# A transformer layer on one core: the expert stretch moved from the 64th to the 80th key block, and the last group's preparation moved up on POOL

## What is computed

```python
xn = layernorm(x)
# attention: 16 heads of 16 numbers, rotary position terms on q and k
q, k, v = rope(xn @ Wq.T) * 16 ** -0.5, rope(xn @ Wk.T), xn @ Wv.T
attn = softmax(where(key > query, -inf, q @ k.T)) @ v
# feed-forward: 32 experts of 128 hidden numbers, 6 of them for each row, and a shared one
w, idx = gate(xn)                      # top 4 of 8 groups, then top 6 experts
y = sum over the 6: w * (silu(xn @ w11[e].T) * (xn @ w33[e].T)) @ w22[e].T
shared = (silu(xn @ sw1.T) * (xn @ sw3.T)) @ sw2.T
out = x + attn @ Wout.T + y + shared
```

## Time and profile before

| | us |
|---|---|
| median of three runs | 979.25 (975.77 to 980.76) |
| the profiled execution, its own time | 968.93 |
| its span in the trace, first to last instruction | 967.2 |
| PE busy | 871.4 |
| DVE busy | 627.8 |
| POOL busy | 525.4 |
| ACT busy | 503.7 |
| mean granted clock of TensorE, share of full speed | 0.959 |

### The profile page before, as it was taken

One profiled execution on the slowest core, in us unless ns is written; L12 is line 12 of the kernel. 1 busy time (PEld: TensorE's weight loads), 2 busy tenths in 40 slices (PEclk: granted clock), 3 DMA queues, 4 the chain that ended last, 5 costly groups with the idle time before them and its releaser, 6 DMA issues.

```text
span 967.2 us, 18271 instructions
## 1 busy us (share of the span) xinstructions
PE 871.4 (90%) x5601; PEld 480.7 (50%) x5602; DVE 627.8 (65%) x1285; ACT 503.7 (52%) x1206; POOL 525.4 (54%) x712
## 2 busy tenths in 40 slices
PE   5788856788999989989999999989999999999997
PEld 3445434333343434367888888854434354443344
DVE  3867665778866687855555555546687867878422
ACT  2322216244666656644444444546666677666662
POOL 2202227968998805236666666628886887830000
PEclk9989877779999999999999999989999999999998
DMA  7000001000000000117777877855552352520011
GB/s 207 1 25 25 25 4 49 17 1 1 1 2 1 2 1 14 37 41 237 218 236 224 237 221 236 135 119 72 72 73 40 49 73 33 72 39 1 6 39 44
DMA packets 55932, 70.93 MB, mean 73 GB/s; under 512 B 11552, under 2 KB 47392, under 8 KB 55840
## 3 DMA queue, kind: packets, MB, share of 16 engines
q0 software_dynamic: 19968, 31.47, 18.3%
q1 hardware_dynamic: 18976, 21.53, 7.4%
q10 hardware_dynamic: 16896, 16.78, 5.1%
HBM read 48.53 MB, written 21.23 MB: 72 GB/s over the span
## 4 chain that ended last, share of the span: by engine, by line
PE 72%; DVE 15%; ACT 4%; issue 3%; DMA 3%; DVEq 2%; SPq 0%; ACTq 0%
PE bank L1116 14%; PE bank L1101 11%; PE vector_banks L1181 11%; PE vector_banks L1081 11%; DVE mpart L886 8%; PE vector_banks L972 7%; PE bank L1194 5%; PE vector_banks L991 3%; PE bank L972 3%; DMA xn_all<-wexp 2%; ACT turned L570 2%; PE bank L991 2%; ACT probs L658 2%; PE vector_banks L1136 2%; PE vector_banks L1084 1%
## 5 line engine op out<-in xcount | busy, mean ns | idle before, releaser
L658 ACT ACTIVATE probs<-bank 128x512 f32<-128x512 f32 (+3 forms) x640 | 312.9, 534 | 221.4 <-PE bank L1101 107.1
L886 DVE TENSOR_REDUCE mpart<-vector_banks 128x2 f32<-128x1024 f32 (+3 forms) x320 | 326.7, 1061 | 93.9 <-PE vector_banks L1081 57.1
L1101 PE MATMUL bank<-turned 99*128 99x512 bf16 (+3 forms) x640 | 208.2, 357 | 13.0 <-ACT probs L658 5.4
L1081 PE MATMUL vector_banks<-turned 96*128 96x512 bf16 (+3 forms) x640 | 185.3, 361 | 17.0 <-DVE mpart L886 13.6
L538 POOL DMA_INDIRECT turned<-normed_rows,tok_i x128 | 125.3, 979 | 90.5 <-PE vector_banks L972 75.9
L553 POOL DMA_INDIRECT res<-expert_rows,slot_i x96 | 148.5, 1547 | 40.0 <-issue 29.9
L1116 PE MATMUL bank<-probs,V 128*32 128x512 f32 (+3 forms) x1280 | 152.6, 547 | 1.6 <-ACT probs L658 1.3
L1101 PEld LDWEIGHTS bank<-turned 99*128 99x128 bf16 x640 | 58.7, 98 | 179.2 <-ACT probs L658 109.3
L1181 PE MATMUL vector_banks<-xn_all,probs 128*128 x512 | 135.3, 387 | 3.5 <-issue 1.5
L484 POOL CAST cat_q<-qk_all 128x512 bf16<-128x512 f32 (+1 forms) x30 | 17.2, 688 | 146.5 <-DVE qk_all L732 98.1
L1181 PEld LDWEIGHTS vector_banks<-xn_all,probs 128*128 128x128 f32 x512 | 87.1, 190 | 16.1 <-issue 8.1
(11 more groups left out here) (153 smaller groups left out, 1003.6 us busy)
## 6 DMA issues: line engine op xcount, KB each, us to landing
expert_rows<-probs ACTq DMA_DIRECT2D x32, 512.0 KB, 4.1
xn_all<-wexp SPq DMA_DIRECT2D x32, 384.0 KB, 4.1
normed_rows<-xn_all SPq DMA_DIRECT2D x4, 512.0 KB, 3.1
turned<-normed_rows,tok_i POOLq DMA_INDIRECT x128, 3.8
out<-res SPq DMA_DIRECT2D x16, 128.0 KB, 1.7
res<-x SPq DMA_DIRECT2D x1, 1536.0 KB, 8.8
res<-expert_rows,slot_i POOLq DMA_INDIRECT x96
probs<-wqkvT SPq DMA_DIRECT2D x1, 768.0 KB, 5.6
```

Source lines behind the costliest of these rows:

```text
L658: A(PT[v // 2 % 4][:, v % 2, 0:width], bank[A_BANK[step][0]][:, 0:width], ACT.Exp).then_inc(s["scalar_bank_read"], 1)
L886: V.tensor_reduce(mpart[:, t % TPC, 2 * j:2 * j + 2, p], ring[:, :, 0:w], AX.X, ALU.max).then_inc(s["vector_bank_read"], 1)
L1081: last = mm(ring[:, h, 0:w], q_turned(slice(0, KQ), 2 * j + h, t * P, P), k_turned(par, slice(0, KQ), 2 * j + h, p * CH, w), start=True, s ...
L1101: last = mm(ring[:, 0:CH - off], k_turned(parity(g), slice(0, KM), h, kb * P, P), q_turned(slice(0, KM), h, c * CH + off, CH - off), start ...
```

## The change

The stretch of expert tiles is put in front of group 2, chunk 0 (block 80) in place of group 1, chunk 3 (block 64). On POOL the first half of group 3 is prepared after the combining of four tiles in place of eight, and the second half after eight in place of twelve. Nothing else changes; the waits inside `prepare_next` and `combine` stay as they are.

```diff
-EXPERTS_AT = (1, NCH - 1)
+EXPERTS_AT = (2, 0)
...
             combine(range(0, 4))
+            prepare_next(3, 0)
             combine(range(4, 8))
-            prepare_next(3, 0)
+            prepare_next(3, 1)
             combine(range(8, 12))
-            prepare_next(3, 1)
             combine(range(12, 16))
```

## The result

The changed kernel takes 986.67 us (median of ten runs, 980.72 to 989.13), the kernel before 977.82 in ten runs taken with them. The ratio is 1.0088, with a 95% interval from 1.0066 to 1.0111: slower by 8.6 us. The prediction was 986.

A forecast was written before the change was run, and what follows sets the result against it. PE was taken to bound the kernel, with POOL's preparation deciding at block 115. POOL's lateness +5.9, clock +1.9 and catching up -0.5 gave +7.3 us on a span of 967.2; 986 us was forecast, eight in ten 978 to 991.

The forecast's parts named there:

- A: Likeliest case: POOL late by 4 to 8 us at block 115, costing +4.5 to +9 us; chance 0.53.
- the restart: PE resuming attention behind the expert stretch: a 4.9 us cost, moved unchanged to blocks 80 to 83, so net 0.
- the wait: At block 115 PE waits 5.8 us for POOL's second half of group 3, ready at 123.6 against 117.8.
- catching up: Behind the wait at block 115, ACT and DVE have caught up on their work, worth 0.5 us gained.
- change of group: ACT's copy of the next values falls into the stretch's start, where ACT has nothing to do: -0.7 us.
- the clock: Behind the wait at block 115, PE's clock falls after idling, costing 1.9 us.
- B: Rival: POOL late by 1 to 3 us, both gaps behind the casts short; +1 to +4, about 982; chance 0.20.
- C: Rival: no wait at block 115, as the gap goes or PE comes slower; -2 to +2, about 979; chance 0.14.
- D: Rival: POOL later still, both gaps long, and the clock; +9 to +13, about 990; chance 0.07.
- E: Rival: restart absorbed in blocks 80 to 83, 4.8 us gained, about 974, if POOL issues transfers faster; chance 0.06.
- Entry: At block 80, before the stretch, DVE's longer last reduces delay the division and PE's first row turn: +0.8 us.
- The expert stretch: The stretch itself, 221.0 us from first row turn to first score step, was expected to keep its length.

The follow-up runs named there:

- second profile: The changed kernel run once more unchanged as a control, against the kernel before: ratio 1.0096, with a 4.96 us wait at block 115.
- the run with the first half sooner: Changed kernel with POOL preparing group 3's first half before its wait for the last expert rows and the combining: 975.13 us, 1.0025 to the kernel before.
- the last experiment: New POOL order and ACT's later store wait at block 64, 969.69 us; beside it, first half prepared before combining plus that wait at block 80, 970.12 us.

## Why the prediction was right

**What held.** The likeliest case, A, came about, by its own steps.

| step | predicted | measured, changed kernel |
|---|---|---|
| first transfer behind the restart | 3.61 | 4.78 |
| last issue of 24 to the first half's end | 18.8 | 17.1 |
| the same, second half | 15.0 | 15.0 |
| restart to second half ready | 123.6 | 122.9 |
| PE at block 115 behind the restart | 117.8 | 117.5 |
| the wait | 5.8 | 5.54 |
| behind the wait, clock less catching up | +1.4 | +2.1 (second profile +1.45) |
| blocks 80 to 83, restart less change of group | +4.2 | +3.3 (second profile +5.2) |

The restart-to-ready time is 826.82 less 703.95; PE's arrival is 826.96 less 5.54 less 703.95. In the second profile POOL was ready at 123.8, PE came at 119.0 and waited 4.96. The 2.1 is block 115's 11.82 us less 4.22 in the kernel before less the wait, and the 1.45 is 10.65 less 4.24 less 4.96. The last row is 14.97 and 16.94 us less the 11.70 of the earlier trace rows. The +1.9 for the clock was right in size: 10 us behind the wait the mean granted clock was 0.76 in the first profile and 0.83 in the second, an estimate of 2.4 and 1.7 us lost. Block 115 took 0.3 us less than that beyond its wait in both, so of the 0.5 for catching up some 0.3 showed. The first half of group 3 was ready at 768.57 for a turn at 778.54, the 10 us early that I had named as a sign.

**Which rivals fell.** B, both gaps short, is out: the first was 3.93 us and some 0.45 more at its end, the second 2.12. With the first transfer 1.2 us later than I counted and the first half 1.7 sooner the errors cancelled, and that was luck. C, no wait, and D, later still, are out by the wait itself. E, the restart absorbed, is out in two ways: the first transfers are issued 1.85 apart as before, and the restart wasn't absorbed in its new place. Measured against the runs in which ACT waits for the store later, it cost 4.7 and 6.7 us at block 80 (14.97 and 16.94 less 10.24), 5.1 and 3.9 at block 64 (18.31 and 17.08 less 13.20), around the 4.9 of the prediction. It is the rival whose other half the later runs bore out: where the restart's cost was really taken away, the changed kernel kept nothing of it until POOL was moved too.

**What was off in size.** *Entry* was put at +0.8 and was 0: from the last score step's start (477.19) to the first row turn 3.45 us, against 3.44 before (420.09 to 423.53); DVE's last long reduce ended at 479.75, just when the division began, 2.54 us behind that step as before. *The change of group* was put at -0.7 and is nearer 0. Blocks 80 to 83 take 11.70 us in the kernel before and 10.2 to 10.8 right behind the stretch with the store wait out of the way; but the first block behind a stretch lacks the values' products of the block ahead of it, which are done at the entry, and blocks 64 to 67 show the same saving, 13.20 us behind the stretch and 14.27 without one. 14.27 + 10.5 is 24.8, 13.20 + 11.70 is 24.9. *The expert stretch* was taken as unchanged. From DVE's first copy of rows to the restart it took 220.5 to 223.8 us in five profiles with the stretch at block 64 (mean 222.4) and 222.9 to 225.6 in seven at block 80 (mean 224.3). And PE's wait at the restart is 2.2 us in all three profiles at block 64 with ACT's old wait, and 3.4 to 4.3 in four at block 80. These two, 1.9 and some 1 us, are about what the run with the first half sooner still stood above the kernel before, 2.4 us with an interval of 0.3 to 4.6. The ranges of the stretch's length overlap, though, and the two kernels of the last experiment, alike but for the place, differ by only 0.4 us, each known to about 1.8 us. Why the stretch and its last store should take longer at block 80 was not found; no run took it apart, and it stays open.

**Luck in the number.** That 986 met 986.67 so closely is partly luck. I added 7.3 us to a base of 979.25; the base measured beside the changed kernel was 977.82, and the change 8.6 to 8.9 us. The two differences have opposite signs. Within the 7.3, the +0.8 of *entry* didn't come, and the time that the stretch took longer wasn't in the sum.

**The profiled span.** Its +11.7 is more than the runs' +8.6. The terms are +4.75 for ACT's unnamed idle time in block 55, +2.3 for the stretch's length, -4.5 for the moved blocks (52.4 in place of 56.87, where I had 52.0), +3.3 for blocks 80 to 83, +0.4 between block 84 and block 115, +7.6 in block 115, which is the term of the prediction, POOL's lateness and what follows it, and -2.1 between the start of block 159 and the end (13.8 us in place of 15.9). The last one varies between 13.8 and 16.4 us over the twelve profiles, with and without the change.

## What to carry to other kernels

When a stretch is moved in one engine's order, write down for every other queue what it must do between that stretch and its next due time: here 48 transfers and two preparations, 123 us, against 118 us of PE's work, and the 5 us short were all lost. A gain made ahead of such a point is worth nothing until the queue that sets it is moved as well, so two edits that measure as next to nothing each (1.0018 and 0.9990 at block 64) were worth 0.4% together. Work of the late queue can go into time in which it sits idle anyway, here its wait for the last store.

## What the runs showed that I had not expected

*A gap behind a batch of indirect transfers.* POOL's first subtraction behind its casts comes after a gap without a releaser: 5.89 us in all four profiles with the first half behind 48 transfers, 3.93 in all five with it behind 24, 2.12 for the second half behind 24 more (2.60 in one profile of nine), 4.07 for a second half behind 48 with the first half done ahead of them, and 1.98 right behind the gathers (both in all three profiles that have them). It goes with the length of the batch and with whether a preparation came since; what it is, no run showed. The Trainium skill (GPSIMD Engine Reference, 2.1 Instruction dispatch) has approximately 6 us for the first call into a freshly loaded kernel; these values are no single such price.

*ACT idle for something unnamed.* Ahead of the stretch, blocks 48 to 55 vary by 5 us between profiles of the same instructions, while from block 84 to the last, waits for POOL apart, no eight blocks vary by more than 0.6 us (the low clock behind such a wait left out too). The end behind the last block varies by 2.6 us again. A single profile of this kernel can't be compared with another's span to better than that; block by block it can.
